# First expert's first layer in two halves of 128 tokens, in a Perceiver block on one core

## What is computed

```python
x = x + _L1_ffn_ref(_layernorm(x, axis=-1), ...)

gate_weights = softmax(x @ Wg + bg)                # 8 experts
topv, topi = top_k(gate_weights, 2)
h = gelu(einsum('bsd,ndh->nbsh', x, W1) + b1)      # 256 -> 512
h = gelu(einsum('nbsh,nhf->nbsf', h, W2) + b2)     # 512 -> 512
eo = einsum('nbsf,nfd->nbsd', h, W3) + b3          # 512 -> 256
out = einsum('nbsd,bsn->bsd', eo, comb)            # comb: top two gate weights
```

## Time and profile before

| what | value |
|---|---|
| median of 3 runs | 515.98 us (515.32 to 516.42) |
| the profiled execution | 515.66 us |
| its span, first to last instruction | 513.7 us |
| mean granted TensorE clock, of full | 0.934 |
| busy share PE / DVE / ACT / POOL | 82% / 66% / 54% / 21% |
| share of PE in the chain of work that ended last | 62% |

### The profile page before, as it was taken

How to read it: one execution, slowest core, us unless ns; L and a number is a source line. 1 busy time by engine, 2 the same in 40 slices (tenths; PEclk the granted TensorE clock), 3 DMA queues, 4 the chain that set the end, 5 groups by cost and what they waited for, 6 DMA issues and landing times.

```text
span 513.7 us, 9021 instructions
## 1 busy us (share of the span) xinstructions
PE 422.1 (82%) x3584; PEld 309.0 (60%) x3584; DVE 340.4 (66%) x544; ACT 275.5 (54%) x613; POOL 108.8 (21%) x76
## 2 busy tenths in 40 slices
PE   0269889978579888765999698998689789999997
PEld 0116556655346566325844373445579689999996
DVE  3698667775664977778236665684653599778772
ACT  4306797756438854553023242466784076777762
POOL 3010653010415100000001326250300113333300
PEclk9999999988858998586999999999799989999999
DMA  6598355661503037006230000005900197540000
GB/s 216 141 280 222 96 130 155 165 165 28 139 1 78 3 103 283 7 1 251 87 153 1 1 0 3 0 1 177 314 2 1 25 355 253 186 165 2 2 1 20
DMA packets 24329, 54.11 MB, mean 105 GB/s; under 512 B 5113, under 2 KB 13529, under 8 KB 20954
## 3 DMA queue, kind: packets, MB, share of 16 engines
q1 hardware_dynamic: 24288, 53.54, 33.6%
HBM read 40.65 MB, written 0.26 MB: 80 GB/s over the span
## 4 chain that ended last, share of the span: by engine, by line
PE 62%; DVE 19%; ACT 10%; issue 6%; DMA 1%; POOL 1%; SPq 0%; ACTq 0%; DVEq 0%; POOLq 0%
PE ps L1297 17%; PE ps L1105 8%; PE ps L918 6%; PE ps L905 5%; ACT reg_b L672 4%; PE ps L874 4%; DVE mx L1678 3%; PE ps L1262 2%; DVE reg_b L1467 2%; PE ps L1013 1%; PE ps L1251 1%; PE ps L1252 1%; PE ps L969 1%; PE ps L1032 1%; DVE bc_split L1451 1%
## 5 line engine op out<-in xcount | busy, mean ns | idle before, releaser
L1678 DVE TENSOR_REDUCE mx<-ps 128x1 f32<-128x1024 f32 x64 | 77.0, 1221 | 45.5 <-PE ps L874 28.9
L672 ACT ACTIVATE reg_b<-ps 128x512 f32<-128x512 f32 x128 | 75.4, 599 | 27.8 <-PE ps L905 16.8
L905 PE MATMUL ps<-qreg,reg_b 98*128 98x128 bf16 x512 | 50.9, 232 | 7.2 <-ACT reg_b L672 5.6
L905 PEld LDWEIGHTS ps<-qreg,reg_b 98*128 98x128 bf16 x512 | 37.6, 104 | 20.1 <-ACT reg_b L672 10.9
L1297 PE MATMUL ps<-part_a 128*128 128x256 f32 x384 | 48.2, 283 | 0.4 <-DVE part_a L1828 0.4
L1105 PE MATMUL ps<-reg_b,xT 128*128 128x512 f32 x96 | 47.6, 618 | 0.0
L1297 PEld LDWEIGHTS ps<-part_a 128*128 128x128 f32 x384 | 46.9, 192 | 0.6 <-DVE part_a L1828 0.6
L918 PE MATMUL ps<-reg_b 128*32 128x128 f32 x1024 | 45.6, 298 | 0.3 <-ACT reg_b L672 0.3
L385 POOL TENSOR_TENSOR rstd<-ve,cf 128x1 f32<-128x1 f32 x12 | 6.8, 565 | 183.6 <-DVE ve L1370 180.5
L874 PE MATMUL ps<-reg_b,qreg 96*128 96x512 bf16 x96 | 35.7, 442 | 11.2 <-DMA reg_b<-reg_b 7.6
L816 ACT ACTIVATE reg_a<-ps,b 128x256 f32<-128x256 f32 x64 | 30.2, 471 | 23.8 <-PE ps L1297 23.7
(11 more groups left out here) (280 smaller groups left out, 864.8 us busy)
## 6 DMA issues: line engine op xcount, KB each, us to landing
reg_b<-in_w SPq DMA_DIRECT2D x16, 512.0 KB, 7.6
reg_b<-in_w SPq DMA_DIRECT2D x8, 1024.0 KB, 7.0
reg_b<-reg_b SPq DMA_DIRECT2D x56, 128.0 KB, 3.3
reg_b<-in_w_qkv SPq DMA_DIRECT2D x3, 2048.0 KB, 7.5
reg_b<-reg_a SPq DMA_DIRECT2D x40, 128.0 KB, 3.2
reg_a<-in_ctxK SPq DMA_DIRECT2D x4, 1024.0 KB, 7.1
reg_a<-in_ctx SPq DMA_DIRECT2D x8, 512.0 KB, 4.8
reg_a<-in_ctxT SPq DMA_DIRECT2D x2, 2048.0 KB, 8.6
```

The lines of the kernel that those rows point to most:

```text
L672: sc.activation(pT[n % 3], score_b[n % 2], ACT.Exp).then_inc(S("exp_done"), 1)
L905: mm = pe.matmul(cols, kS[g % 3][0:SROWS, c // 8, j, P * (c % 8):P * (c % 8 + 1)], qT[b][0:SROWS, HPG * hg + j, :], start=not last, stop=True)
L1678: ve.reduce_max(mx[:, piece // 2, piece % 2:piece % 2 + 1], score_a[m % 2].rearrange("p i k -> p (i k)"), X_AXIS).then_inc(S("max_done"), 1)
```

## The change

The first expert's first layer is taken out of `hidden1` and becomes `first_hidden(b)`, run once for each batch on 128 token columns instead of once on 256. PE's order becomes: transposes, gate products and first layer of b0, then the same of b1. DVE splits b0 between the statistics and the normalising of b1. The transposes of b1 and its gate scores get PSUM places of their own (banks 6 and 7), since bank 4 is now written by b0's products; so the wait for the gate scores to be read (`g_shift`) moves from the first layer's last bank to the first expert's `expert_out`. All else is unchanged.

```diff
@@ -248,6 +248,11 @@
         side = ps[:, 6, 256:512]
+
+        def columns_at(t, b):
+            return side if (t, b) == (1, 0) else bank(1, 2, D) if (t, b) == (5, 1) else bank(b, 0, D)
+
+        gate_scores = [bank(0, 1, NE), bank(1, 3, NE)]
...
             def transposed_x(t, b):
                 sc.wait_ge(S(f"xT_ps{b}"), t)
-                src = side if (t, b) == (1, 0) else bank(b, 0, D)
+                src = columns_at(t, b)
...
             def x_to_columns(t, b):
                 pe.wait_ge(S(f"xn_done{b}"), t + 1)
-                dst = side if (t, b) == (1, 0) else bank(b, 0, D)
+                dst = columns_at(t, b)
...
-            for b in range(NB):
-                pe.wait_ge(S(f"x_done{b}"), 5)
-                x_to_columns(5, b)
-            pe.wait_ge(S("ffn_in"), 64)
-            for b in range(NB):
-                pe.wait_ge(S(f"xT_sb{b}"), 5)
-                for k in range(KD):
-                    mm = pe.matmul(bank(b, 1)[:, 0:NE], xT[b][:, k, :], wg[:, k, :], start=k == 0, stop=k == KD - 1)
-                mm.then_inc(S("g_ps"), 1)
-
...
+            def gate_products(b):
+                pe.wait_ge(S("ffn_in"), 64)
+                pe.wait_ge(S(f"xT_sb{b}"), 5)
+                for k in range(KD):
+                    mm = pe.matmul(gate_scores[b], xT[b][:, k, :], wg[:, k, :], start=k == 0, stop=k == KD - 1)
+                mm.then_inc(S("g_ps"), 1)
+
+            def first_hidden(b):
+
+                w = high[0][0], low[0][0]
+                half = slice(P * b, P * (b + 1))
+                pe.wait_ge(S("w_low"), 1)
+                pe.wait_ge(S("x_split"), b + 1)
+                for m in range(MF):
+                    mm = products(ps[:, 2 + m, half],
+                                  (([part[:, k, P * m:P * (m + 1)] for part in w], (x_high[:, k, half], x_low[:, k, half]))
+                                   for k in range(KD)))
+                    if b == NB - 1:
+                        mm.then_inc(S("h1_ps"), 1)
+
             def hidden1(e):
...
-                    if e >= 1:
-                        pe.wait_ge(S("h2_sb"), MF * (e - 1) + m + 1)
-                    elif m == MF - 1:
-                        pe.wait_ge(S("g_shift"), NB)
+                    pe.wait_ge(S("h2_sb"), MF * (e - 1) + m + 1)
...
                 for b in range(NB):
                     if e >= 1:
                         pe.wait_ge(S("eo_added"), NB * (e - 1) + b + 1)
+                    else:
+                        pe.wait_ge(S("g_shift"), NB)
...
-            pe.wait_ge(S("x_split"), NB)
+            for b in range(NB):
+                pe.wait_ge(S(f"x_done{b}"), 5)
+                x_to_columns(5, b)
+                gate_products(b)
+                first_hidden(b)
             for e in range(NE):
-                hidden1(e)
+                if e >= 1:
+                    hidden1(e)
...
-            for b in range(NB):
+            def add4(b):
                 ve.wait_ge(S("o4_ps"), b + 1)
                 ve.tensor_tensor(x[b][:, :], bank(b, 0, D), x[b][:, :], ALU.add).then_inc(S(f"x_done{b}"), 1)
-                ln_stats(5, b)
-                ln_apply(5, b)
-
-
-            for b in range(NB):
+
+            def split_x(b):
                 half = slice(P * b, P * (b + 1))
                 ve.wait_ge(S(f"xT_sb{b}"), 5)
                 link(ve.tensor_copy(x_high[:, :, half], xT2[:, :, half]))
                 ve.tensor_tensor(x_low[:, :, half], xT2[:, :, half], x_high[:, :, half], ALU.subtract)\
                     .then_inc(S("x_split"), 1)
+
+            add4(0)
+            ln_stats(5, 0)
+            ln_apply(5, 0)
+            add4(1)
+            ln_stats(5, 1)
+            split_x(0)
+            ln_apply(5, 1)
+            split_x(1)
             for b in range(NB):
                 ve.wait_ge(S("g_ps"), b + 1)
-                link(ve.tensor_tensor(logit[b][:, 0:NE], bank(b, 1, NE), bg[:, :], ALU.add))
+                link(ve.tensor_tensor(logit[b][:, 0:NE], gate_scores[b], bg[:, :], ALU.add))
```

## The result

| | before | with the change |
|---|---|---|
| median of 22 runs, us | 515.91 | 520.01 |
| ratio, with its 95% interval | | 1.0101 (1.007 to 1.0133) |
| the profiled execution's span, us | 513.7 | 517.2 |
| stage, from DVE's second add to the first of the 648 products, us | 20.96 | 25.10 |

The change makes the kernel **slower by 1.0%**, 5.2 us (3.6 to 6.9). The ratio is taken from the executions outside a slower state, the medians from all 22, so the 4.1 us between the medians is another figure. The direction was forecast; the size forecast was 2.6. Within the profiled execution the loss lies in the one stage that the change touches: behind it both kernels run the same 648 products in 77.96 us. The stage is 4.1 us longer; the span grows by 3.5, since DVE's second add came 0.6 us earlier in this execution.

What follows compares the result with a forecast made beforehand. Bound: normalising b1, its transposes, copy, split and gate scores, then 3.3 us of ACT, then PE nearly without a gap. Later PE run 1.1 plus one half-clock spell 1.5 make 2.6: 518.6 us on the median, range 516.3 to 520.4.

Steps and rivals of the forecast that it cites:

- Split of b0: DVE, ahead of normalising b1: split done at 410.08, normalising some 0.15 us late; 0.8 more if a cast caught it.
- Price of a 128-column product: PE's first layer: 0.11 us each, paced by the weight load; 24 products take 2.64 us.
- The two bounds, 0.06 and 0.22: PE's first layer: 0.060 us is half a 256-column product, 0.22 a plain 128-column product; 1.44 to 5.3 us per half.
- their rivals: PE's first layer: half price, no slower, 516.0, chance 0.10; plain price, 3.8 us slower, 519.8, chance 0.27.
- the rival of the plain price: PE's first layer: a 128-column product costs 0.22 us like a plain one; 3.8 us slower, 519.8; chance 0.27.
- Transposes, scores, continuous PE run: From b1's transposes to the 648 products: transposes 1.54 us late, gate scores 1.15, PE's continuous run 1.1.
- The collision of POOL's third cast: POOL's cast now falls on DVE's `lower_weights`; if it holds them up by 1.18 us, 0 to 0.6 reach the path.
- so PE stays ahead: Second half of the first layer: 24 products end near 417.1, ahead of ACT's Gelus with rounding, 0.8 us each.
- The clock: PE's first half or second layer's start: one half-clock spell on the path, 1.5 us; 0 with none, 3.0 with two.
- one of the three signs named: Wrong if transposes follow normalising within 0.4 us, first Gelu by 416.3, or the chain runs through PE's whole first layer.
- the load-bound price: PE's first layer: 0.11 us per 128-column product, set by loading its 128 x 128 weights; with one spell, chance 0.38.
- The range: Whole kernel: 516.3 to 520.4 us, from load-bound price with shorter hand-overs to plain price with part of a spell.

Runs made afterwards that it cites:

- run 3: Changed kernel plus filler products of 256 columns, results unread, where PE idles; stage 22.24 us, ratio 1.0024 to the kernel before.
- run 5: Kernel before, first layer as 48 products of 128 columns in the old order, 16 and 5 filler products around b1's transposes; stage 21.41 us, ratio 1.0033.
- run 1: Changed kernel with each of the 48 first-layer products streaming its 128 columns twice (256 columns); stage 23.94 us, ratio 1.0068 to the kernel before.
- run 2: Kernel before with the first layer's 24 products of 256 columns as 48 of 128, order as before; stage 26.56 us, ratio 1.0088.
- run 7: Kernel before with 16 filler products between the transposes, then also 5 behind b1's; stages 20.96 and 20.97 us, ratio of the first 1.001.
- run 6: Kernel before with only DVE's split of b0 moved ahead of normalising b1; stage 21.15 us, ratio 1.0.
- run 9: Changed kernel, unchanged, profiled twice more; stages 26.63 and 26.61 us.

## Why the prediction was wrong

It had the direction and what the change costs at full clock, and one term of the sum, the clock, too small by a factor of two to three. With that term it also lost the path behind b1's transposes. By its steps:

- **Split of b0: right.** The first product was forecast 2.12 us behind the second add (410.12 against 408.00); it came at 2.10 (409.49 against 407.39). The split was not caught by a cast. Normalising b1 kept its 1.10 and began 1.97 us behind the add, as before; the 0.15 of delay did not come.
- **Price of a 128-column product: right, at full clock.** 0.11 was taken, 0.112 measured (runs 3 and 5). Halving the columns saves 7% of 0.120, so the columns do not set the pace; that the load sets it, as the prediction argued, fits this, but no run varied the load. The two bounds, 0.06 and 0.22, fall with their rivals. In the changed kernel's own profile the spacing is some 0.21, which looks like the rival of the plain price; the granted clock of 0.50 beside it and the 0.112 of run 3 say that it is the clock. The Trainium skill (TensorE: Matmul & The Clock Gate, LDWEIGHTS) gives P / 1.2 ns to load weights of P columns, 107 ns for 128, which agrees with the 0.112 at full clock. The 56 ns that the prediction took from its section Back-to-back issue gap holds for an isolated product; the same section says that it has no budget for the weight load and gives some 81 ns for a stream with loads. The 0.112 measured lies above both.
- **Transposes, scores, continuous PE run: right, at full clock.** Forecast 1.54, 1.15 and 1.1 us late; in run 3, 1.58, 1.16 and 1.28. The collision of POOL's third cast is in it, but `lower_weights` kept its 3.42 us; the cast held up the first `lower_hidden`, 1.26 us. In the changed kernel itself "so PE stays ahead" did not hold: at half clock ACT's fourth Gelu waited 0.36 us for PE.
- **The clock: this step failed.** It read "Both ends: 0 with no spell, 3.0 with two. I take one.", at 1.5 us a spell. It took the *length* of a spell from the kernel before, where products of 256 columns ran in it, and assumed the same length for products of 128. Runs 1 and 2 show that the length depends on what runs: with 256 columns from the start the full clock was back after 3.3 us (run 1), with 128 it did not come back while they ran, 9.5 us without a pause (run 2), and the spells became 13.5 to 17 us long. The term is 25.10 - 22.24 = 2.9 us in the first profile and 4.4 in the other two, 3.9 on average; with the order's 1.3 that is 5.2. Nor did the spell fall on one of the two places named, the first half or the start of the second layer, but on both and on all between.
- **What would show it wrong:** one of the three signs named came. The chain of waits now runs through PE's first layer from end to end. With 0.112 at full clock it is not a sign against the load-bound price; in run 3, at full clock, the chain goes over ACT's table and Gelus again.
- **The range: luck, as far as it held.** The median of 520.01 lies inside 516.3 to 520.4, but 515.98 + 5.2 does not, and the upper part of the range stood on the plain price, which fell.

What stays open: why the clock fell when it did, and how much of the second layer it takes until it is back. PE had been idle for some of the time ahead of every fall, but 16 and 5 filler products around b1's transposes did not prevent the fall in run 7, while the same 16 and 5 did in run 5.

## What to carry to other kernels

Halving the columns of a product that brings its own 128 x 128 weights halved nothing here: at full clock it cost 0.112 us against 0.120, so two halves cost nearly double, and in an engine's fixed order the first half delays whatever stands behind it (b1's transposes by 1.6 us at full clock, by 3.6 in the changed kernel's own profile). Before splitting work to fill an engine's idle time, look whether the engine that fills up stands on the path right after. And when the granted clock is at half, do not take the length of that spell from other work: see what PE runs in it.

## What the runs showed of the hardware that was not expected

At half clock, products followed each other at 0.21 us whether they streamed 128 or 256 columns. While products of 128 columns ran, a clock that had fallen did not come back in any of these profiles, not in 9.5 us of unbroken work either (run 2). Counted from the first product of 256 columns at half clock, it was back after 2 to 5 us: 2.0 in the changed kernel's first profile, 3.3 in the kernel before and in run 1, 4.1 in run 6, 4.8 in run 9. At full clock, 48 products of 128 columns in a row, 5.4 us, did not make it fall (run 5). So PE that the profile shows busy without a break stayed at 1.2 GHz for 13.5 us, and more columns per product, even useless ones, made the stage shorter: 23.94 us against 25.10 to 26.63.
